# Repeated matmuls in TensorE's waits, and DMA signals split by consumer, in a two-layer decoder kernel

## What is computed

```python
x = _layernorm(x + _L0_attn_ref(x, ...))          # attention with a compressive memory, 4 x 8 heads of 8
x = _layernorm(x + _L0_xattn_ref(x, ctx, ...))    # rotary cross attention over channels, 8 heads
x = _layernorm(x + _L0_ffn_ref(x, ...))           # 8 experts, 2 for each token, 256 -> 1024 -> 256
x = _layernorm(x + _L1_attn_ref(x, ...))          # 16 heads, values from a triangular solve, causal softmax
x = _layernorm(x + _L1_xattn_ref(x, ctx, mask, ...))
x = _layernorm(x + _L1_ffn_ref(x, ...))           # 8 families of experts with low-rank terms, and a shared expert
```

```python
def expert(...):
    xe = x + w @ muW.T
    gate = silu(_fused_linear(xe, gW, gqa, gqb, gs, w))
    up = _fused_linear(xe, uW, uqa, uqb, us, w)
    return _fused_linear(gate * up, dW, dqa, dqb, ds, w)
y = einsum('fth,tf->th', outs, scalar)
```

## Time and profile before

| | us |
|---|---|
| median of 3 runs | 1113.26 |
| lowest and highest run | 1110.69, 1115.44 |
| the profiled execution's own time | 1109.19 |
| span of the profiled execution (first to last instruction) | 1107.4 |
| mean granted TensorE clock, share of full | 0.931 |
| PE busy | 972.9 (88%) |
| DVE busy | 550.2 (50%) |
| ACT busy | 362.3 (33%) |
| POOL busy | 200.1 (18%) |

### The profile page before, as it was taken

One profiled execution on the slowest core, in us unless ns is written; L12 is line 12 of the kernel. 1 busy time (PEld: TensorE's weight loads), 2 busy tenths in 40 slices (PEclk: granted clock), 3 DMA queues, 4 the chain that ended last, 5 costly groups with the idle time before them and its releaser, 6 DMA issues.

```text
span 1107.4 us, 18950 instructions
## 1 busy us (share of the span) xinstructions
PE 972.9 (88%) x7488; PEld 608.9 (55%) x7488; DVE 550.2 (50%) x1110; ACT 362.3 (33%) x724; POOL 200.1 (18%) x241
## 2 busy tenths in 40 slices
PE   7998879998899999983963899898498999999996
PEld 4664523333468899981452467758364444444443
DVE  2599788885431111015578576536762333233324
ACT  3444346666222233321366354143231000000002
POOL 5021000000012222210026841041000111111110
PEclk9999869999799999995987799998898999999998
DMA  6000000000745455523000202030015022221101
GB/s 235 2 2 1 1 1 2 2 2 1 276 141 180 149 186 188 170 86 115 1 1 1 76 2 97 1 136 3 1 47 119 13 87 87 81 77 66 37 1 38
DMA packets 27242, 75.15 MB, mean 68 GB/s; under 512 B 9860, under 2 KB 17292, under 8 KB 21780
## 3 DMA queue, kind: packets, MB, share of 16 engines
q1 hardware_dynamic: 24948, 67.91, 18.2%
q0 software_dynamic: 2208, 6.03, 1.8%
HBM read 67.48 MB, written 6.46 MB: 67 GB/s over the span
## 4 chain that ended last, share of the span: by engine, by line
PE 70%; DVE 21%; issue 3%; DMA 3%; ACT 3%; SPq 0%; POOL 0%; DVEq 0%; ACTq 0%; POOLq 0%
PE psum L1521 8%; PE psum L1096 8%; PE psum L1108 7%; DVE arena L2082 4%; PE psum L819 3%; PE psum L1525 3%; PE psum L1287 3%; PE psum L1551 3%; PE psum L1509 2%; PE psum L1555 2%; PE psum L1000 2%; DVE arena L2001 2%; DVE arena L2000 2%; PE psum L1546 2%; PE psum L1257 2%
## 5 line engine op out<-in xcount | busy, mean ns | idle before, releaser
L1944 ACT ACTIVATE arena<-psum 128x512 f32<-128x512 f32 (+1 forms) x32 | 19.0, 593 | 227.6 <-PE psum L1525 227.6
L1521 PE MATMUL psum<-arena 128*128 128x512 f32 (+1 forms) x192 | 90.6, 608 | 0.5 <-DVE arena L2530 0.5
L1762 ACT ACTIVATE arena<-psum,arena 128x128 f32<-128x128 f32 x184 | 52.4, 368 | 115.4 <-PE psum L1096 99.1
L2082 DVE TENSOR_REDUCE arena<-psum 128x2 f32<-128x512 f32 x128 | 82.6, 688 | 15.2 <-PE psum L946 13.1
L1096 PE MATMUL psum<-arena 128*128 128x128 f32 x736 | 86.7, 276 | 0.0
L1096 PEld LDWEIGHTS psum<-arena 128*128 128x128 f32 x736 | 84.0, 192 | 2.7 <-issue 2.7
L745 POOL TENSOR_TENSOR arena<-arena 128x512 f32<-128x512 f32 (+1 forms) x32 | 40.4, 1264 | 241.9 <-ACT arena L1944 241.9
L1108 PE MATMUL psum<-arena 128*128 x368 | 83.1, 379 | 0.0
L2229 DVE COPY arena<-psum 128x256 f32<-128x256 f32 x23 | 9.8, 425 | 135.6 <-PE psum L1081 85.2
L1739 ACT ACTIVATE arena<-psum 128x1024 f32<-128x1024 f32 x64 | 65.4, 1024 | 35.4 <-PE psum L968 32.5
L1108 PEld LDWEIGHTS psum<-arena 128*128 128x128 f32 x368 | 68.2, 190 | 8.4
(11 more groups left out here) (371 smaller groups left out, 1818.9 us busy)
## 6 DMA issues: line engine op xcount, KB each, us to landing
arena<-in_w SPq DMA_DIRECT2D x31, 1024.0 KB, 12.5
arena<-in_experts SPq DMA_DIRECT2D x8, 1248.0 KB, 5.9
arena<-mixed SPq DMA_DIRECT2D x16, 256.0 KB
arena<-mixed SPq DMA_DIRECT2D x8, 512.0 KB
arena<-in_ctx SPq DMA_DIRECT2D x2, 1024.0 KB, 7.4
arena<-returned SPq DMA_DIRECT2D x8, 256.0 KB, 5.0
arena<-in_w_xattn SPq DMA_DIRECT2D x1, 1538.5 KB, 9.9
arena<-in_w_ffn SPq DMA_DIRECT2D x1, 1152.0 KB, 5.2
```

The costliest lines, as they stand in the source:

```text
L1521: pe.matmul(out, e[w][:, k, :], xe6[:, half, k, :], start=(k == 0), stop=False)
L1762: last = act.activation(hidt[:, r % 2, ic * P:(ic + 1) * P], bank(n)[:, i * P:(i + 1) * P], ACT.Gelu, bias=b1_tile[:, r % 4, ic:ic + 1])
L2082: ax_max.by(dve.tensor_reduce(nmx[:, b % 2, :, h], bank(u % 2).rearrange("p (t s) -> p t s", t=2), AX.X, ALU.max, negate=True))
```

## The change

A helper on PE multiplies the 128 x 128 identity by itself four times side by side (512 columns) into a bank that holds nothing at that time. Its result is read by nobody. The default identity is the float32 one; `ident16` is bfloat16. The helper is called at ten places, with the counts in the diff; there is no wait in it. The counts add up to 108 float32 repeats (8, 2, 6, 3 in the last round of the cross attention, 5, 17, 35, 3 behind the early scores, 29) and 14 in bfloat16.

The signals of the mixtures are split: `near_in` counts the two DMAs into `wm6`, `mix_in` the two into `we6`, `scale_in` the one into `scale6`, and the DMAs are issued in that order. `fuse_in(0)` and `ranks(0)` move ahead in PE's stream.

```diff
+        near_in = [Signal(loaded[n].sem, 32) for n in ("ident", "w_attn0", "w_xattn0")]
+        scale_in = [Signal(loaded[n].sem, base) for n, base in (("consts", 32), ("consts_late", 32), ("w_route0", 16))]
...
             def fetch_mix(f):
-                done, mixed = mix_in[f % BUFS], a["mixed"]
-                w = wide(mixed[f * KX:(f + 1) * KX, :], 1, RX)
+                mixed, buf = a["mixed"], f % BUFS
+                few = mixed[f * KX:(f + 1) * KX, :]
+                for k in range(KC):
+                    sp.dma_start(wm6[32 * k:32 * k + KX, buf, :], few).then_inc(near_in[buf].sem, 16)
                 for half in range(2):
-                    sp.dma_start(we6[64 * half:64 * half + 64, f % BUFS, :], w).then_inc(done.sem, 16)
-                sp.dma_start(scale6[:, f % BUFS, :], mixed[FX * KX + f:FX * KX + f + 1, :].to_broadcast([P, B * S]))\
-                  .then_inc(done.sem, 16)
-                for k in range(KC):
-                    sp.dma_start(wm6[32 * k:32 * k + KX, f % BUFS, :], mixed[f * KX:(f + 1) * KX, :]).then_inc(done.sem, 16)
+                    sp.dma_start(we6[64 * half:64 * half + 64, buf, :], wide(few, 1, RX)).then_inc(mix_in[buf].sem, 16)
+                sp.dma_start(scale6[:, buf, :], mixed[FX * KX + f:FX * KX + f + 1, :].to_broadcast([P, B * S]))\
+                  .then_inc(scale_in[buf].sem, 16)
...
+            def keep_clock(count, spare, eye=ident):
+
+                for _ in range(count):
+                    pe.matmul(bank(spare), eye, wide(eye, 1, BANK // P), start=True, stop=True)
...
                 if b >= 3 and b % 2 == 1:
                     turn_out0(b // 2 - 1)
+            keep_clock(8, 3)
...
             for u in range(NT, 2 * NT + 1):
                 if u < 2 * NT:
                     project(u)
+                if u == NT + 1:
+                    keep_clock(2, 3)
                 if u > NT:
                     replicate(u - 1)
+            keep_clock(6, 3)
             pe.wait_ge(st_ready.sem, 4 * NT)
...
                     first_scores_x(u, tc)
+                keep_clock(1, 5, ident16)
                 if u == HX:
                     turn_max(0)
...
+                    if b == B and p >= 1:
+                        keep_clock(1, 5)
                     if p == 1:
                         if b >= 1:
                             turn_out_x(b - 1)
...
+            keep_clock(5, 5)
             turn_x(1)
...
+            keep_clock(17, 0)
             for j in range(NT + 1):
                 if j < NT:
                     turn_heads1(j)
...
             for w in range(EARLY_W):
                 scores1(w)
+                if w == 0:
+                    keep_clock(35, 5)
                 if w >= 1:
                     turn_probs1(w - 1)
+                    keep_clock(1, 5)
...
-                    pe.wait_ge(mix_in[f % BUFS].sem, 16 * MIX_DMAS * (f // BUFS + 1))
+                    pe.wait_ge(near_in[f % BUFS].sem, near_in[f % BUFS].base + 32 * (f // BUFS + 1))
...
+            keep_clock(29, 5)
             turn_x(4)
...
             pe.wait_ge(wt6_sb.sem, wt6_sb.base + 2)
+            pe.wait_ge(sh_h.sem, sh_h.base + 2 * len(SHARED) - 1)
+            fuse_in(0)
             shared_down(1, (0, 1))
+            ranks(0)
+            shared_down(1, (2, 3))
             pe.wait_ge(tail_blank.sem, 1)
-            for step in range(-1, STEPS + 1):
+            for step in range(STEPS + 1):
                 if step + 1 < STEPS:
                     fuse_in(step + 1)
-                if step == -1:
-                    shared_down(1, (2, 3))
```

More of the change, by code:

```diff
@@ L478, in build @@
         mix_in = [signal(f"mix_in_{i}") for i in range(3)]
-        MIX_DMAS = 5
+        near_in = [Signal(loaded[n].sem, 32) for n in ("ident", "w_attn0", "w_xattn0")]
+        scale_in = [Signal(loaded[n].sem, base) for n, base in (("consts", 32), ("consts_late", 32), ("w_route0", 16))]
         scaled6 = signal("scaled6")
@@ L740, in _ @@
                 if half == 0:
-                    pool.wait_ge(mix_in[f % BUFS].sem, 16 * MIX_DMAS * (f // BUFS + 1))
+                    pool.wait_ge(scale_in[f % BUFS].sem, scale_in[f % BUFS].base + 16 * (f // BUFS + 1))
                 cols = slice(half * BANK, (half + 1) * BANK)
@@ L2535, in ranks6 @@
                 if half == 0:
-                    dve.wait_ge(mix_in[f % BUFS].sem, 16 * MIX_DMAS * (f // BUFS + 1))
+                    dve.wait_ge(mix_in[f % BUFS].sem, 32 * (f // BUFS + 1))
                 dve.wait_ge(mid_ps.sem, mid_ps.base + ring[("a", 0), n] + 1)
```

## The result

| | before | changed |
|---|---|---|
| median of 4 runs each, side by side | 1113.76 | 1127.43 |
| lowest and highest | 1110.69, 1115.44 | 1126.71, 1131.26 |
| the profiled execution's own time | 1109.19 | 1126.71 |
| span of the profiled execution | 1107.4 | 1124.9 |
| mean granted TensorE clock | 0.931 | 0.973 |

A forecast was written before the change was run, and what follows sets the result against it. The prediction took PE to bound the kernel; 0.9 + 0.9 - 2.1 + 4.1 + 12.6 + 10.7 - 8.4 = +18.7 us on 1109.2 gave 1127.9, and 4.1 more to the median gave 1132, range 1122 to 1141.

The forecast's parts named there:

- early scores: 35 + 3 repeats from 596.6 end at 626.6 against 612.62: overrun +14.0, clock gain -1.4, net +12.6 us.
- The sum: Net of the places and the mixtures: +18.7 us on the profiled execution's 1109.2, giving 1127.9.
- The price of a repeat: On PE, a float32 repeat takes two rows of 0.43 us, 0.86 us at full clock.
- the rival of one row: A repeat costs one row, 0.43 us, so no wait is overrun and the change is faster: 1093; chance 0.05.
- The overruns: Repeats that outlast PE's waits push everything behind them, since PE is next on the chain as each wait ends.
- first scores: Ahead of them 6 repeats end at 144.9 against 142.59: +2.3, clock gain -1.4, net +0.9 us.
- heads: Turned heads: 17 repeats from 554.7 end at 569.3 against 562.67, +6.6; gains -1.7 and -0.8, net +4.1 us.
- last `turn_x`: Ahead of it 29 repeats from 790.1 end at 815.0 against 803.11: +11.8, less 1.1, net +10.7 us.
- What the clock gives back: Full clock shortens PE's work behind the repeats: 1.4 first scores, 1.7 and 0.8 heads, 1.4 early scores, 1.1 `turn_x`.
- The mixtures: Small DMAs issued first and moved calls let `features(0)` start at 850.7 instead of 859.07: -8.4 us.
- The stretches set at zero: Stretches no step named, forecast 0; behind the early scores PE runs without a gap for 16 rounds, nothing caught up.
- The step from the execution to the median: Before's median lay 4.1 us above its profiled execution, so 1127.9 became an expected median of 1132.

The follow-up runs named there:

- the second execution of before: The kernel before, unchanged, profiled a second time: one run, 1114.2 us, span 1112.4.
- the mixtures alone: The changed kernel without any repeat, so only split signals, new DMA order and moved calls: 1105.17 us, ratio 0.9953 to before.
- the signals alone: The kernel before with split signals and new DMA order, `fuse_in(0)` and `ranks(0)` left in their places: one run, 1111.32 us.
- the kernel with more places: The kernel of half the counts with 35 further float32 repeats at six places: 1089.95 us, ratio 0.9791 to before.
- the second execution of the changed kernel: The changed kernel, unchanged, profiled a second time: one run, 1126.2 us, span 1124.4.
- the first experiments: Runs including the mixtures alone (1105.17 us), beside which before had a median of 1109.45 us over 12 runs.
- the kernel of half the counts: The changed kernel with float32 counts cut to 4, 1, 3, 3, 9, 18, 15 and the last single repeat dropped: 1100.21 us, ratio 0.9915 to before.
- the kernel of half the counts without bfloat16 repeats: The kernel of half the counts with the 14 bfloat16 repeats among the first scores removed: 1092.78 us, ratio 0.9848 to before.

## Why the prediction held, and where it was off

The forecast was 1132 us, slower, between 1122 and 1141; the median is 1127.43. The sum was made against one profiled execution: 18.7 us against the 17.5 measured. The stretches that it named came to 19.5, and those it had set at zero to -1.9, so a part of that nearness is luck.

**The price of a repeat** held: 0.86 us, two rows of 0.43. That the counts fit a price of one row was right as well. Halving the columns at the same counts made a kernel of 1093.6, where the rival of one row had been worked out at 1093.

**The overruns** held to 0.3 us each: first scores 2.6 for a forecast of 2.3, heads 6.7 for 6.6, early scores 14.2 for 14.0, last `turn_x` 11.8 for 11.8. That nothing hides them was shown twice: the last `turn_x` started 11.8 us sooner behind the last output when 14 repeats were left out, and DVE stood for 15 us.

**What the clock gives back** held too: 1.45 for 1.4 in the first scores, 2.15 for 2.5 behind the heads, 1.35 for 1.4 behind the early scores, 1.35 for 1.1 behind `turn_x`. That the clock holds through the transposes of the last `turn_x` was assumed against a rule of the Trainium skill (TensorE: Matmul & The Clock Gate, Part 4: PE-mode transpose: the full clock doesn't engage for them). The windows of the changed kernel over those transposes have 1.00:

```profile
830.10:834.00 3.90, 2.97 (x22) 2.12 (x21) 0.00 (x0) 2.54 (x8) 0.00 (x0) 1.00 0.00 0
```

By the rule the sum would have been some 4 us higher; here the trace does not agree with it. But the prediction also read from one row that transposes had raised the clock, at 808.1, and that the other traces don't bear out. In the second execution of before, in the mixtures alone and in the signals alone the clock stayed at 0.50 through the same transposes and through 11 us of gates and `gate_up` behind them. What raised it at 808.1 in the first is open. The fall inside `turn_x(2)` at 512.8 in the kernel with more places is a case in which the rule would have been a fair warning.

**The mixtures** held: -8.1 for -8.4. The run of the signals alone puts 6.95 of it on the signals and the order of the DMAs, with the full clock that follows when the wait is gone. One reading was off at no cost: `we6` was to land about in time for `ranks6(0)`, and in the changed kernel DVE waited 1.98 us for it, while PE's next rows followed without a gap:

```profile
873.27 0.69 DVE L2559 TENSOR_TENSOR arena<-psum,arena 128x512 f32<-128x512 f32 x1 [1.98 <-DMA arena<-mixed]
```

**The stretches set at zero** were off. From the first chunk of the solve to the last output, -4.4 us. The step that failed there reads "Behind it PE runs without a gap for 16 rounds, and nothing can be caught up." For the 16 rounds it held: the changed kernel stayed 19.6 us behind until 687.5 of before's time. Behind them before had three low stretches, from 688.6, 719.3 and 756.9, and the changed kernel none, though no repeat stands there: 0.3, 1.3 and 2.8 us were caught up at them. The pair loop went the other way, +1.8, with a low stretch from 158.7 to 165.6 in it. That is not the change's own, since the second execution of the changed kernel had -1.1 there. Of the first, by windows:

```profile
145.60:158.70 13.10, 12.41 (x77) 4.04 (x76) 12.43 (x23) 4.31 (x6) 0.00 (x0) 1.00 0.01 1
158.70:165.60 6.90, 6.53 (x64) 2.08 (x62) 3.72 (x8) 3.14 (x4) 0.00 (x0) 0.51 0.00 0
```

With +0.7 in the experts, these come to -1.9.

**The step from the execution to the median** is most of why the number was 4.6 us too high: 3.4 of it, the other 1.2 being the sum's. It added 4.1 because before's runs lay above its profiled execution, but the changed kernel's profiled execution (1126.71) was only 0.7 under its own median. Before's scatter goes with the clock: of its 12 runs beside the first experiments, the fastest (1106.69) had 0.935 and the slowest (1115.81) 0.924. One such difference was traced. The second execution of before lost 4.8 us of its 5.0 behind the last `turn_x`, where the changed kernel has 1.00. That the other runs of before lost theirs in places that the repeats fill is likely but not shown. A difference that the change itself takes away should not have been added to it.

**Open** is why the stretch from the first chunk to the last output ran wholly at 1.00 in both executions of the changed kernel, and only partly so in before and in the others (1.7 to 4.1 us less than in before's first execution, by kernel; 2.8 and 2.9 in the two that are the same program up to there). No run changed the work ahead of it alone.

## What to carry to other kernels

Work out the price of a filler from rows of the same form and type in the trace, and count how many rows one instruction becomes; then set the counts a little under each wait, since here every microsecond too many cost a full one, while one too few only left a short wait. Place them by more than one profiled execution, as the low stretches move. Where several engines wait for one count over several DMAs, give each its own signal and issue first what is needed first; here the two were only tried together. When a change removes the cause of the scatter between runs, compare medians and don't carry the old scatter over.

## What the runs showed of the chip

- A float32 matmul of 512 columns takes 0.86 us at full clock, as two rows; of 256 columns 0.43 (15.2 us for 35), as two rows of 0.22.
- The same kernel, run twice, had the low clock in partly different stretches. One such difference, behind the last `turn_x`, was worth 5 us of 1110. The seven runs of before beside the kernel with more places spread over 12 us (1106.78 to 1118.81), the four of that kernel over 3.5.
- One bfloat16 repeat for each unit held the clock at 1.00 through float16 scores that use 32 rows of the array; without them it was 0.50 (146 to 150 us).
- Twenty microseconds of repeats held the clock only as far as 512.8, in the transposes of `turn_x(2)`, where it fell to 0.51 for 3.5 us. In the last `turn_x`, behind 25 us of them, it held, and in `turn_x(1)` of the kernel of half the counts without bfloat16 repeats too. What makes these differ was not tried.
